# Layer 1 of a group's first two batches, spread over the last four attention slots through a spare PSUM bank

## The chip, the cores and the metric

The kernel runs on one core of a Trainium2 chip. Its engines are TensorE (PE in the profile, its weight loads PEld), VectorE (DVE), ScalarE (ACT), GpSimd (POOL) and SyncE (SP), which issues the DMAs. Each works off its own instructions in order and waits on semaphores. The metric is the device time of one execution in microseconds (us), lower is better.

## The reference, cut to what matters

There are 64 batches of 256 tokens with 256 features, and for each batch 120 context vectors. Attention has 16 heads of 16 features.

```python
x = x + attention(layernorm(x), ctx, mask) @ W_out.T    # softmax(10 * tanh(q k / 4)) v, masked keys out
f = layernorm(x)
gf = global_net(mean of f over the tokens)              # 3 small layers, one value per batch
out = f
for _ in range(3):
    h = gelu(out @ w1 + b1); h = gelu(h @ w2 + b2); h = gelu(h @ w3 + b3)
    tf = sigmoid(h @ w4 + b4)                           # one value per token
    coupling = 0.1 + adaptive_range * (0.7 * gf + 0.3 * tf - 0.5) * 2
    out = out + coupling * twist(out)                   # twist permutes and negates quarters of the features
x = x + out
```

## The kernel before

The batches are worked through in 8 groups of 8. For each batch there is an attention slot; after the eight slots that finish a group's features comes that group's feed-forward stage ("ffn", all three cycles for its 2048 tokens in 4 chunks of 2 batches), and then the next slots. The functions of every engine are called in a fixed order by a loop over `slots()`. In slot `i` the scores are made for batch `i`, the weighted values for `i-1`, the projection for `i-2`, and the second norm and the feature transpose for `i-3` (`LAG = 3`). The place of a slot in its group is `(i - LAG) % GROUP`, 0 to 7. The ffn stage of a group stands behind its place 7.

**Attention slot.** ScalarE: tanh of half of batch `i` (L880), exp of the second half of `i-1` (L886), tanh of the other half, exp, and `features` (L896), which writes `f_t` and the sum over tokens; in place 7 one more exp. TensorE: scores half 0 (L1116), weighted values half 0 (L1132), query transposes (L1091), scores half 1, projection half 0 (L1147), key transposes (L1100), weighted values half 1, projection half 1, feature transposes (L1160). A half of the scores takes all of the banks 0 to 3 and so waits for the tanh before it. VectorE: `attn_out` of half 0 (L678), `queries_out` (L664), stats, the combination of an output of the group before, `high_half` in places 2 and 4, `keys_out` (L669), `attn_out` of half 1, the division, a transpose, the residual and stats of `i-2`. GpSimd: the norms, two products per output of the group before (L511, L520), `query_hat` (L435), and last `low_half` (L529).

**Layer 1.** The first layer's product is taken once for each chunk and updated by linearity in the cycles: `u = w1' f` and `v = w1' twist(f)`. To be precise enough, `f` and the weights are split into two float16 parts each (`high_half` on VectorE, `low_half` on GpSimd, buffer `f_hl` with two slots) and three partial products are added in PSUM. `layer1_twisted` (L1179) makes `v` in banks 2 and 3, `layer1_straight` (L1192) makes `u` in banks 0 and 1, each 12 matmuls of 512 columns. `twisted_out` (L924) and `straight_out` (L934) on ScalarE scale them into `v_t` and, in place of the features, into `f_t`. `gelu1` (L912) of the first cycle reads PSUM, later ones read `f_t`.

**The head of an ffn stage.** TensorE: both products of chunk 0, the global net's first layer (L1254), the twisted product of chunk 1, the global net's second layer (L1258), layer 2 (L1205) of chunk 0, and so on. ScalarE: two evictions, two gelus (with a table load, as exp and gelu have different tables), two evictions, the global net's gelu (L999), the evictions of chunk 1. GpSimd: norms for queries of later batches, `low_half` of chunk 2, one more query, `low_half` of chunk 3.

Weighted values use banks 4 and 5, one for each half; layer 2 uses the same two in turn.

Of the kernel before, what the change touches and what calls it, by code (L numbers as in the profile page):

```python
# [35 lines left out]
P = 128  # L36
# [8 lines left out]
def xattn_ffn_kernel(nc, x, ctx, mask, W_out, scale, log_C,  # L45
# [30 lines left out]
    with ExitStack() as stack:  # L76
# [108 lines left out]
        PV_BANKS = (4, 5)  # L185
# [46 lines left out]
        s_uv = sem("s_uv")  # L232
        s_h1 = sem("s_h1")
# [17 lines left out]
        LOW_AT = (3, 4, 5, 6)  # L251
# [67 lines left out]
        def groups_before(i):  # L319

            return (i - LAG) // GROUP

# [261 lines left out]
        def _(eng):  # L584
# [88 lines left out]
            def attn_out(b, n):  # L673

                eng.wait_ge(s_pv, 2 * b + n + 1)
                if b >= 2:
                    eng.wait_ge(s_on, b - 1)
                eng.transpose(o_t[:, b % 2, 2 * n:2 * n + 2].rearrange("p c q r -> p (c q r)"),  # L678
                              banks(PV_BANKS[n])).then_inc(s_ot, 1)

# [45 lines left out]

            def couple(g, p):

                turn, chunk = UPDATES * g + p, slot_of(p)[1]
                eng.wait_ge(s_th, turn + 1)  # L730
                eng.wait_ge(s_gcs, g + 1)
                for b in range(CB):
                    c = coup[:, turn % 2, b * S:(b + 1) * S]
                    eng.tensor_scalar(c, c, c_tok[:, 0:1], c_batch[:, chunk * CB + b:chunk * CB + b + 1],  # L734
                                      ALU.mult, ALU.add).then_inc(s_coup, 1)

            def update_both(g, p):
# [5 lines left out]
                eng.wait_ge(s_uv, 2 * EK * (number + 1))  # L743
# [57 lines left out]
            for kind, i in slots():  # L801
                if i == 2 and kind == "attention":
                    split_weights()
                if kind == "attention":
# [16 lines left out]
                    if 0 <= nxt < NB:  # L821
                        keys_out(nxt)
                    if 0 <= here < NB:
                        attn_out(here, 1)
                        divide(here)
                        attn_features(here)
# [45 lines left out]
        def _(eng):  # L872
# [26 lines left out]
            def gelu1(g, p):  # L899
# [3 lines left out]
                for m in range(EK):  # L903
                    if cyc == 0:
                        eng.wait_ge(s_w, n_weights)
                        eng.wait_ge(s_vec0, N_SPLIT)
# [69 lines left out]
            for kind, i in slots():  # L976
# [15 lines left out]
                else:  # L992
                    early = i * GROUP + GROUP + LAG
                    glob = banks(TR_BANK)[:, SMALL_AT:SMALL_AT + 3 * GROUP]
                    twisted_out(i, 0)
                    gelu1(i, 0)
                    straight_out(i, 0)
# [53 lines left out]
        def _(eng):  # L1051
# [52 lines left out]
            def scores(b, n):  # L1104
# [3 lines left out]
                if n == 0 and after_ffn(b):  # L1108
                    eng.wait_ge(s_th, UPDATES * groups_before(b))
                    eng.wait_ge(s_uv, 2 * EK * CHUNKS * groups_before(b))  # L1110
                elif 2 * b + n:
                    eng.wait_ge(s_tanh, 2 * b + n)
# [8 lines left out]
            def weighted_values(b, n):  # L1121
# [3 lines left out]
                if after_ffn(b + 1):  # L1125
                    eng.wait_ge(s_h2, PASSES * groups_before(b + 1) - 1 + n)
                elif b:
                    eng.wait_ge(s_ot, 2 * (b - 1) + n + 1)
                for c in (2 * n, 2 * n + 1):
                    for j in range(HG):  # L1130
                        h = n * HALF + 2 * j + c % 2
                        last = eng.matmul(banks(PV_BANKS[n])[j * SLOT:(j + 1) * SLOT, (c % 2) * S:(c % 2 + 1) * S],  # L1132
# [33 lines left out]

            def layer1_twisted(g, chunk):
# [3 lines left out]
                eng.wait_ge(s_vec0, N_SPLIT)  # L1171
                eng.wait_ge(s_flo, EK * (number + 1))
                for m in range(EK):
                    if chunk == 0:
                        eng.wait_ge(s_tanh, 2 * min(GROUP * g + GROUP + LAG, NB))
                    else:
                        eng.wait_ge(s_uv, 2 * EK * (number - 1) + m + 1)
# [5 lines left out]
            def layer1_straight(g, chunk):  # L1183
# [3 lines left out]
                for m in range(EK):  # L1187
                    if chunk:
                        eng.wait_ge(s_h1, EK * (PASSES * g + chunk - 1) + m + 1)
                        eng.wait_ge(s_uv, 2 * EK * (number - 1) + EK + m + 1)  # L1190
# [5 lines left out]
            def layer2(g, p):  # L1196
# [4 lines left out]
                else:  # L1201
                    eng.wait_ge(s_ot, 2 * min(GROUP * g + GROUP + LAG - 1, NB))
                for k in range(EK):
# [15 lines left out]
            def layer4(g, p):  # L1219
# [7 lines left out]
                if paired(p):  # L1227
                    eng.wait_ge(s_uv, 2 * EK * CHUNKS * (g + 1))
# [36 lines left out]
            for kind, i in slots():  # L1265
                if kind == "attention":
# [3 lines left out]
                    if i != early:  # L1270
# [94 lines left out]
```

## Time and profile before

| | |
|---|---|
| median of 3 runs | 1096.31 us (1096.15 to 1098.32) |
| the profiled execution | 1098.4 us, its span 1096.6 us |
| TensorE busy | 979.9 us (89%), weight loads 530.3 us (48%) |
| ScalarE busy | 920.6 us (84%) |
| VectorE busy | 808.9 us (74%) |
| GpSimd busy | 554.1 us (51%) |
| chain that ended last | ScalarE 41%, TensorE 30%, issue 13%, VectorE 10% |
| mean granted clock of TensorE | 0.979 of full speed |

The shares are means over two alternating kinds of stage, attention and ffn, of some 67 and 63 us for a middle group, with different limits. The chain is followed back from the last instruction; "issue" is time for which the profile shows no wait.

### The profile page before, as it was taken

Reading aid. Unit: us, or ns where it says so; the run is one execution under the profiler, and the core shown is the slowest. Engines: PE = TensorE matmul, PEld = TensorE weight load, DVE = VectorE, ACT = ScalarE, POOL = GpSimd, SP = SyncE. Lnnn points to the kernel's source line nnn. Section 1 sums busy time; section 2 is a strip of 40 time slices with the busy share of each in tenths; the row PEclk is TensorE's granted clock in tenths of the full one; section 3 lists DMA queues with packets and bytes.
Section 4 is the critical chain, followed back from the end, with each engine's and each line's share of the span. In section 5 each row is a group of like instructions: output and inputs, shape, how many; then the busy total and the mean of one; then the engine's idle time right before and its main releaser. Section 6 shows DMA issues by size and latency. Waiting matters only on the chain.

```text
span 1096.6 us, 21849 instructions
## 1 busy us (share of the span) xinstructions
PE 979.9 (89%) x7260; PEld 530.3 (48%) x7260; DVE 808.9 (74%) x1738; ACT 920.6 (84%) x1153; POOL 554.1 (51%) x1053
## 2 busy tenths in 40 slices
PE   6899989899998999999999998989999899896993
PEld 4455435554355544554345543555435554453431
DVE  3888596985868666885869849698487867687285
ACT  3899778997799977998789977899779997795675
POOL 3367504884068810897028950488406881078104
PEclk7899999999999999999999999999999999998997
DMA  5433001430034200441005310143003420021002
GB/s 119 82 58 61 1 2 39 105 86 0 2 72 100 58 1 2 96 92 41 2 1 121 90 19 2 40 104 86 0 2 73 99 58 1 1 53 40 0 1 78
DMA packets 191119, 51.71 MB, mean 47 GB/s; under 512 B 165920, under 2 KB 174624, under 8 KB 191008
## 3 DMA queue, kind: packets, MB, share of 16 engines
q1 hardware_dynamic: 191008, 50.31, 21.6%
q8 instruction: 60, 0.98, 0.4%
q14 instruction: 51, 0.42, 0.1%
HBM read 33.37 MB, written 16.78 MB: 46 GB/s over the span
## 4 chain that ended last, share of the span: by engine, by line
ACT 41%; PE 30%; issue 13%; DVE 10%; SPq 2%; POOL 2%; DMA 1%; DVEq 0%; ACTq 0%; POOLq 0%
ACT probs L880 18%; ACT probs L886 14%; PE ps L1205 7%; PE ps L1192 6%; PE ps L1179 5%; ACT f_t L896 4%; PE ps L1116 3%; PE ps L1235 2%; DVE move_u L747 2%; DVE move_v L749 2%; PE ps L1214 2%; ACT h L912 2%; DVE f_t L753 2%; DVE coup L734 2%; PE ps L1147 1%
## 5 line engine op out<-in xcount | busy, mean ns | idle before, releaser
L880 ACT ACTIVATE probs<-ps,u_scale 120x2048 f32<-120x2048 f32 x128 | 257.6, 2012 | 21.4 <-PE ps L1116 21.4
L886 ACT ACTIVATE probs<-probs,exp_bias,clip 120x2048 f32<-120x2048 f32 x128 | 275.0, 2149 | 0.1
L1205 PE MATMUL ps<-h,w 128*128 128x512 f32 x384 | 184.4, 606 | 12.9 <-ACT h L912 12.1
L1116 PE MATMUL ps<-q_t,k_t 32*120 32x256 f32 x2048 | 150.0, 407 | 34.6 <-ACT probs L880 33.1
L475 POOL TENSOR_TENSOR c<-tok_c 128x16 f32<-128x16 f32 x8 | 1.8, 224 | 329.3 <-issue 329.3
L1147 PE MATMUL ps<-wo_t,of_t 128*128 128x256 f32 x512 | 144.5, 405 | 1.8 <-DVE xy L703 1.8
L678 DVE STREAM_TRANSPOSE o_t<-ps 128x512 f32<-128x512 f32 x128 | 90.8, 709 | 74.5 <-PE ps L1132 74.2
L1132 PE MATMUL ps<-probs,va 120*32 120x256 f32 x2048 | 138.4, 388 | 2.0 <-ACT probs L886 2.0
L1116 PEld LDWEIGHTS ps<-q_t,k_t 32*120 32x120 f32 x2048 | 95.1, 181 | 65.0 <-issue 60.5
L1147 PEld LDWEIGHTS ps<-wo_t,of_t 128*128 128x128 f32 x512 | 87.3, 190 | 51.0 <-issue 42.1
L1205 PEld LDWEIGHTS ps<-h,w 128*128 128x128 f32 x384 | 66.8, 188 | 87.7 <-issue 64.4
L942 ACT ACTIVATE h<-ps,b 128x512 f32<-128x512 f32 x96 | 65.6, 684 | 39.1 <-PE ps L1205 39.1
L912 ACT ACTIVATE h<-f_t,b 128x512 f32<-128x512 f32 x128 | 85.1, 715 | 11.6 <-DVE f_t L772 8.2
L1179 PE MATMUL ps<-f_hl,w1t_hl 128*128 128x512 f16 x384 | 90.1, 385 | 0.0
L734 DVE TENSOR_SCALAR coup<-coup,c_tok,c_batch 128x256 f32<-128x256 f32 x128 | 49.3, 427 | 54.7 <-ACT coup L966 53.6
L1192 PE MATMUL ps<-f_hl,w_hl 128*128 128x512 f16 x384 | 88.2, 379 | 0.0
L529 POOL TENSOR_TENSOR f_hl<-f_t,f_hl 128x512 f16<-128x512 f32 x64 | 75.2, 1186 | 19.9 <-DVE f_hl L725 19.9
L1132 PEld LDWEIGHTS ps<-probs,va 120*32 120x32 f32 x2048 | 53.8, 110 | 57.5 <-issue 19.5
L435 POOL TENSOR_SCALAR q_hat<-xy,neg,rstd 128x256 f32<-128x256 f32 x128 | 77.4, 613 | 4.2 <-POOL rstd L425 3.8
L456 POOL TENSOR_SCALAR f_hat<-xy,neg,rstd 128x256 f32<-128x256 f32 x128 | 74.4, 587 | 5.4 <-POOL rstd L446 5.4
L725 DVE CAST f_hl<-f_t 128x1024 f16<-128x1024 f32 x32 | 23.6, 738 | 70.0 <-PE ps L1192 70.0
L912 ACT ACTIVATE h<-ps,b,uv_scale 128x512 f32<-128x512 f32 x64 | 48.9, 776 | 31.2 <-PE ps L1192 31.1
(128 smaller groups left out, 1826.5 us busy)
## 6 DMA issues: line engine op xcount, KB each, us to landing
xy<-in_x_dram SPq DMA_DIRECT2D x64, 256.0 KB, 3.3
out_dram<-xy SPq DMA_DIRECT2D x64, 256.0 KB, 2.0
cbuf<-in_ctx_dram SPq DMA_DIRECT2D x64, 120.0 KB, 2.8
va<-in_ctx_dram SPq DMA_DIRECT2D x64, 120.0 KB, 3.6
tok_c<-coup SPq DMA_DIRECT2D x256, 0.5 KB, 2.0
move_v<-in_L_xattn_W_out_dram SPq DMA_DIRECT2D x1, 256.0 KB, 5.6
move_u<-in_L_ffn_cn_w_dram SPq DMA_DIRECT2D x1, 256.0 KB, 3.4
w<-in_L_ffn_cn_w_dram SPq DMA_DIRECT2D x1, 128.0 KB, 3.1
```

Source lines behind the costliest of these rows:

```text
L435: eng.tensor_scalar(q_hat[:, at, t, :], xy[:, b % XR, t * E:(t + 1) * E], neg1[:, at, t:t + 1], rstd1[:, at, t:t + 1], ALU.add, ALU.mult). ...
L529: eng.tensor_tensor(f_hl[:, slot, 1, k], f_t[:, k, tok], f_hl[:, slot, 0, k], ALU.subtract) \
L678: eng.transpose(o_t[:, b % 2, 2 * n:2 * n + 2].rearrange("p c q r -> p (c q r)"), banks(PV_BANKS[n])).then_inc(s_ot, 1)
L880: eng.activation(probs[:, b % 2, n * HALF:(n + 1) * HALF, :].rearrange("k h q -> k (h q)"), banks(SCORE_BANK, 4)[0:KEYS, :], ACT.Tanh, sca ...
L886: eng.activation(p, p, ACT.Exp, scale=clip[0:KEYS, 0:1], bias=exp_bias[:, b:b + 1]).then_inc(s_exp, 1)
L912: eng.activation(h1[:, p % 2, m, :], source, ACT.Gelu, bias=b1[:, m:m + 1], scale=by) \
L1116: last = eng.matmul(banks(SCORE_BANK + r)[0:KEYS, odd * S:(odd + 1) * S], k_t[rows, b % 2, odd, n, :], q_t[rows, b % 2, n, :], start=True, ...
L1132: last = eng.matmul(banks(PV_BANKS[n])[j * SLOT:(j + 1) * SLOT, (c % 2) * S:(c % 2 + 1) * S], va[:, b % VR, h, :], probs[:, b % 2, h, :], ...
L1147: last = eng.matmul(banks(X_BANK)[:, t * E:(t + 1) * E], of_t[:, k, t * P:(t + 1) * P], wo_t[:, k, :], start=(k == 0), stop=(k == EK - 1))
L1179: last = eng.matmul(banks(V_BANKS[m]), w1t_hl[:, w, k, m * P:(m + 1) * P], halves[:, f, k, :], start=(n == 0), stop=(n == len(PRODUCTS) - 1))
L1192: last = eng.matmul(banks(U_BANKS[m]), w1_hl[:, w, k, m * P:(m + 1) * P], halves[:, f, k, :], start=(n == 0), stop=(n == len(PRODUCTS) - 1))
L1205: last = eng.matmul(banks(bank), w2[:, k, :], h1[:, p % 2, k, :], start=(k == 0), stop=(k == EK - 1))
```

## The change

Chunk 0 of every group no longer gets its layer 1 in the ffn stage. Its four pieces (`v` and `u`, two halves of the features each: six matmuls and one eviction a piece) are made one by one in the attention slots of places 4 to 7, by `layer1_side` on TensorE between the queries and the second half of the scores, and by `side_out` on VectorE between `keys_out` and the second `attn_out`. They pass through bank 5. That bank is free because both halves of the weighted values now go through bank 4, each behind the transpose of the one before. `gelu1` of chunk 0 reads `f_t`; `twisted_out` and `straight_out` of chunk 0 (ScalarE) and both products of chunk 0 (TensorE) leave the head. The low halves of chunk 0 are made in places 2 and 3 instead of 3 and 4.

```diff
-        PV_BANKS = (4, 5)
+        PV_BANK = 4
+        SIDE_BANK = 5
...
         HIGH_AT = (2, 4)
-        LOW_AT = (3, 4, 5, 6)
+        LOW_AT = (2, 3, 5, 6)
+
+        SIDE_AT = (4, 5, 6, 7)
+        SIDES = 2 * EK
...
+        def uv_done(g, chunk):
+            return 2 * EK * ((CHUNKS - 1) * g + chunk)
...
+        def side_of(i):
+            at = (i - LAG) % GROUP
+            return SIDE_AT.index(at) if i >= LAG and at in SIDE_AT else None
...
+            def side_out(g, part):
+                kind, m = part // EK, part % EK
+                eng.wait_ge(s_vec0, N_SPLIT)
+                eng.wait_ge(s_l1, 2 * EK * CHUNKS * g + part + 1)
+                if g and kind == 0:
+                    eng.wait_ge(s_vupd, EK * (CHUNKS * (g - 1) + 1))
+                    eng.wait_ge(s_mvu, EK * (UPDATES * (g - 1) + CHUNKS + 1))
+                dst = (v_t, f_t)[kind]
+                eng.tensor_scalar(dst[:, m, 0:CT], banks(SIDE_BANK), uv_scale[:, 0:1], None, ALU.mult).then_inc(s_side, 1)
...
                     if 0 <= nxt < NB:
                         keys_out(nxt)
+                    if side_of(i) is not None:
+                        side_out((i - LAG) // GROUP, side_of(i))
                     if 0 <= here < NB:
                         attn_out(here, 1)
...
                 for m in range(EK):
-                    if cyc == 0:
+                    if cyc == 0 and chunk == 0:
                         eng.wait_ge(s_w, n_weights)
-                        eng.wait_ge(s_vec0, N_SPLIT)
+                        eng.wait_ge(s_side, SIDES * (g + 1))
+                        source, by = f_t[:, m, 0:CT], 1.0
+                    elif cyc == 0:
                         eng.wait_ge(s_l1, 2 * EK * (CHUNKS * g + chunk) + EK + m + 1)
                         source, by = banks(U_BANKS[m]), uv_scale[:, 0:1]
...
                     glob = banks(TR_BANK)[:, SMALL_AT:SMALL_AT + 3 * GROUP]
-                    twisted_out(i, 0)
                     gelu1(i, 0)
-                    straight_out(i, 0)
...
                 eng.wait_ge(s_va[b % VR], 16 * (b // VR + 1))
-                if after_ffn(b + 1):
-                    eng.wait_ge(s_h2, PASSES * groups_before(b + 1) - 1 + n)
-                elif b:
-                    eng.wait_ge(s_ot, 2 * (b - 1) + n + 1)
+                if after_ffn(b + 1) and n == 0:
+                    eng.wait_ge(s_h2, PASSES * groups_before(b + 1) - 1)
+                if 2 * b + n:
+                    eng.wait_ge(s_ot, 2 * b + n)
...
+            def layer1_side(g, part):
+                kind, m = part // EK, part % EK
+                halves = f_hl[:, CHUNKS * g % 2]
+                weights = (w1t_hl, w1_hl)[kind]
+                if part == 0:
+                    eng.wait_ge(s_vec0, N_SPLIT)
+                    eng.wait_ge(s_flo, EK * (CHUNKS * g + 1))
+                if part == 0 and g:
+                    eng.wait_ge(s_h2, PASSES * g)
+                elif part:
+                    eng.wait_ge(s_side, SIDES * g + part)
+                for n, (w, f, k) in enumerate(PRODUCTS):
+                    last = eng.matmul(banks(SIDE_BANK), weights[:, w, k, m * P:(m + 1) * P], halves[:, f, k, :],
+                                      start=(n == 0), stop=(n == len(PRODUCTS) - 1))
+                last.then_inc(s_l1, 1)
...
                         if 0 <= nxt < NB:
                             queries(nxt)
+                        if side_of(i) is not None:
+                            layer1_side((i - LAG) // GROUP, side_of(i))
                         if 0 <= i < NB:
                             scores(i, 1)
...
                     early = i * GROUP + GROUP + LAG
-                    layer1_twisted(i, 0)
-                    layer1_straight(i, 0)
                     global_net(i, 0)
```

The other lines of the diff fit the counts of `s_uv`, which chunk 0 no longer raises, let chunk 1's products wait for the last tanh alone, and let layer 2's first two products and the first update wait for `s_side`.

## Rows read from the trace of the kernel before

**Rows 1.** Windows: a stretch's us, then busy us (instructions) of each engine

```profile
core 0: us, PE busy (x) PEld busy (x) DVE busy (x) ACT busy (x) POOL busy (x), PEclk, DMA share, GB/s
338.20:346.59 8.39, 7.55 (x90) 4.83 (x86) 7.31 (x17) 8.39 (x10) 8.01 (x14) 1.00 0.52 126
381.50:388.66 7.16, 7.16 (x35) 3.72 (x36) 0.83 (x2) 5.19 (x9) 5.81 (x11) 1.00 0.01 3
...
1016.00:1018.00 2.00, 2.00 (x6) 0.76 (x5) 0.00 (x0) 0.27 (x2) 0.00 (x0) 0.50 0.00 0
```

**Rows 2.** Timeline of TensorE, places 4 to 7 of group 2: start, us, engine, line

```profile
338.88 0.66 PE L1091 MATMUL ps<-ident,q_hat 128*128 128x128 f32 x4
340.37 1.14 PE L1116 MATMUL ps<-q_t,k_t 32*120 32x256 f32 x16 [0.84 <-ACT probs L880]
...
348.78 1.14 PE L1116 MATMUL ps<-q_t,k_t 32*120 32x256 f32 x16 [0.85 <-ACT probs L880]
...
356.42 0.66 PE L1091 MATMUL ps<-ident,q_hat 128*128 128x128 f32 x4 [0.66 <-POOL q_hat L435]
...
364.94 0.66 PE L1091 MATMUL ps<-ident,q_hat 128*128 128x128 f32 x4 [0.77 <-POOL q_hat L435]
```

**Rows 3.** Timeline of ScalarE: place 7 and head of group 2, last features

```profile
367.20 2.10 ACT L880 ACTIVATE probs<-ps,u_scale 120x2048 f32<-120x2048 f32 x1
...
373.74 1.41 ACT L924 ACTIVATE v_t<-ps,uv_scale 128x512 f32<-128x512 f32 x2
375.17 1.28 ACT L912 ACT_TABLE_LOAD   x1
376.46 1.45 ACT L912 ACTIVATE h<-ps,b,uv_scale 128x512 f32<-128x512 f32 x2
377.80 1.26 ACT L934 ACTIVATE f_t<-ps,uv_scale 128x512 f32<-128x512 f32 x2
378.94 0.28 ACT L999 ACTIVATE gh<-ps,gb 128x8 f32<-128x8 f32 x1
...
1015.80 0.38 ACT L896 ACTIVATE f_t<-ps 128x256 f32<-128x256 f32 x1
```

**Rows 4.** Timeline of TensorE, the head of group 2

```profile
370.34 2.75 PE L1179 MATMUL ps<-f_hl,w1t_hl 128*128 128x512 f16 x12
372.93 2.75 PE L1192 MATMUL ps<-f_hl,w_hl 128*128 128x512 f16 x12
...
379.49 1.98 PE L1205 MATMUL ps<-h,w 128*128 128x512 f32 x4
...
385.00 2.76 PE L1179 MATMUL ps<-f_hl,w1t_hl 128*128 128x512 f16 x12
```

**Rows 5.** Groups of instructions by line: busy us and mean ns behind the bar

```profile
L912 ACT ACTIVATE h<-f_t,b 128x512 f32<-128x512 f32 x128 | 85.1, 715 | 11.6 <-DVE f_t L772 8.2 <-PE ps L1205 3.4
...
L912 ACT ACTIVATE h<-ps,b,uv_scale 128x512 f32<-128x512 f32 x64 | 48.9, 776 | 31.2 <-PE ps L1192 31.1
```

**Rows 6.** Timeline of VectorE, place 7 of group 2

```profile
365.69 0.65 DVE L664 COPY q_t<-ps 128x512 f32<-128x512 f32 x1
...
369.08 0.72 DVE L678 STREAM_TRANSPOSE o_t<-ps 128x512 f32<-128x512 f32 x1 [0.37 <-PE ps L1132]
```

**Rows 7.** Timeline of GpSimd, place 3 of group 2 to its head

```profile
333.50 0.32 POOL L422 TENSOR_SCALAR var<-mv 128x2 f32<-128x2 f32 x1 [0.59 <-DVE mv L658]
...
339.55 1.15 POOL L529 TENSOR_TENSOR f_hl<-f_t,f_hl 128x512 f16<-128x512 f32 x1
...
379.69 2.27 POOL L529 TENSOR_TENSOR f_hl<-f_t,f_hl 128x512 f16<-128x512 f32 x2
```

**Rows 8.** Timeline of TensorE, place 7 of group 0 and head of group 7

```profile
105.29 1.14 PE L1116 MATMUL ps<-q_t,k_t 32*120 32x256 f32 x16 [0.85 <-ACT probs L880]
...
1015.18 4.62 PE L1179 MATMUL ps<-f_hl,w1t_hl 128*128 128x512 f16 x12
...
1025.53 1.98 PE L1205 MATMUL ps<-h,w 128*128 128x512 f32 x4
```

More of the change, by code:

```diff
@@ L232, in xattn_ffn_kernel @@
         s_uv = sem("s_uv")
+        s_side = sem("s_side")
         s_h1 = sem("s_h1")
@@ L678, in attn_out @@
                 eng.transpose(o_t[:, b % 2, 2 * n:2 * n + 2].rearrange("p c q r -> p (c q r)"),
-                              banks(PV_BANKS[n])).then_inc(s_ot, 1)
+                              banks(PV_BANK)).then_inc(s_ot, 1)
             def divide(b):
@@ L742, in update_both @@
                 eng.wait_ge(s_coup, CB * (turn + 1))
-                eng.wait_ge(s_uv, 2 * EK * (number + 1))
+                if chunk == 0:
+                    eng.wait_ge(s_side, SIDES * (g + 1))
+                else:
+                    eng.wait_ge(s_uv, uv_done(g, chunk))
                 eng.wait_ge(s_upd, EK * turn)
@@ L903, in gelu1 @@
                 for m in range(EK):
-                    if cyc == 0:
+                    if cyc == 0 and chunk == 0:
                         eng.wait_ge(s_w, n_weights)
-                        eng.wait_ge(s_vec0, N_SPLIT)
+                        eng.wait_ge(s_side, SIDES * (g + 1))
+                        source, by = f_t[:, m, 0:CT], 1.0
+                    elif cyc == 0:
                         eng.wait_ge(s_l1, 2 * EK * (CHUNKS * g + chunk) + EK + m + 1)
@@ L1109, in scores @@
                     eng.wait_ge(s_th, UPDATES * groups_before(b))
-                    eng.wait_ge(s_uv, 2 * EK * CHUNKS * groups_before(b))
+                    eng.wait_ge(s_uv, uv_done(groups_before(b), 0))
                 elif 2 * b + n:
@@ L1131, in weighted_values @@
                         h = n * HALF + 2 * j + c % 2
-                        last = eng.matmul(banks(PV_BANKS[n])[j * SLOT:(j + 1) * SLOT, (c % 2) * S:(c % 2 + 1) * S],
+                        last = eng.matmul(banks(PV_BANK)[j * SLOT:(j + 1) * SLOT, (c % 2) * S:(c % 2 + 1) * S],
                                           va[:, b % VR, h, :], probs[:, b % 2, h, :], start=True, stop=True,
@@ L1170, in layer1_twisted @@
                 halves = f_hl[:, number % 2]
-                eng.wait_ge(s_vec0, N_SPLIT)
                 eng.wait_ge(s_flo, EK * (number + 1))
                 for m in range(EK):
-                    if chunk == 0:
+                    if chunk == 1:
                         eng.wait_ge(s_tanh, 2 * min(GROUP * g + GROUP + LAG, NB))
                     else:
-                        eng.wait_ge(s_uv, 2 * EK * (number - 1) + m + 1)
+                        eng.wait_ge(s_uv, uv_done(g, chunk - 2) + m + 1)
                     for n, (w, f, k) in enumerate(PRODUCTS):
@@ L1187, in layer1_straight @@
                 for m in range(EK):
-                    if chunk:
+                    if chunk > 1:
                         eng.wait_ge(s_h1, EK * (PASSES * g + chunk - 1) + m + 1)
-                        eng.wait_ge(s_uv, 2 * EK * (number - 1) + EK + m + 1)
+                        eng.wait_ge(s_uv, uv_done(g, chunk - 2) + EK + m + 1)
                     for n, (w, f, k) in enumerate(PRODUCTS):
@@ L1202, in layer2 @@
                     eng.wait_ge(s_ot, 2 * min(GROUP * g + GROUP + LAG - 1, NB))
+                    eng.wait_ge(s_side, SIDES * (g + 1))
                 for k in range(EK):
@@ L1227, in layer4 @@
                 if paired(p):
-                    eng.wait_ge(s_uv, 2 * EK * CHUNKS * (g + 1))
+                    eng.wait_ge(s_uv, uv_done(g, CHUNKS - 1))
                 for b in range(CB):
```

## The prediction

> **What bounds the kernel now.** I read the windows of a stretch of one middle group first, then the timelines of TensorE, ScalarE, GpSimd and VectorE over it. I call an attention slot by its place, 0 to 7, in its group; in the group of the rows, places 4 to 7 begin at 338.20, 346.59, 354.98 and 363.37 us and the last ends at 371.75. In place 4 ScalarE is busy for all of 8.39 us [rows 1]: attention is bound by it, and what delays it there is never made up. TensorE is next. Its steps follow each other without a gap, but for one wait a slot: 0.84 and 0.85 us for a tanh in places 4 and 5, 0.66 and 0.77 us for q_hat in places 6 and 7 [rows 2]. VectorE too is nearly full. In the feed-forward stage TensorE is busy for the whole of 381.50 to 388.66 [rows 1]. Between the two lies a head of ScalarE work: two evictions, a table load, two gelus, two evictions, then the global net's first gelu, for which TensorE waits before layer 2 at 379.49 [rows 3, 4].
>
> **What the change takes out.** Of ScalarE's head it takes the two evictions at 373.74 (to 375.17: 1.43 us) and the two at 377.80 (to 378.94: 1.14 us) [rows 3]. The gelus read f_t instead of PSUM: 715 ns against 776 ns in the line groups [rows 5], so 0.12 us for two. Together 2.69 us. On TensorE 24 matmuls leave the head, but that time was not limiting there: TensorE began them at 370.34, before ScalarE was through with exp at 373.74, and still waited for ScalarE later. So a middle group's head saves 2.69 us, not the 5.2 us of matmuls. After layer 2 the order is the old one and bound by TensorE, so what the head gives lasts.
>
> **What it adds to the slots.** (a) TensorE: six matmuls of 512 columns in each of places 4 to 7. From the start of twelve at 370.34 to that of the next twelve at 372.93 pass 2.59 us [rows 4] (the 2.75 us of the row hold a modelled tail), so six cost 1.30 us. They stand between the queries and the second half of the scores, just where TensorE waits today. (b) VectorE: one 128x512 scaling out of PSUM, 0.65 us by the q_t copy of that shape [rows 6]; it stands after keys_out and ahead of attn_out, where VectorE waits 0.37 us for TensorE [rows 6]. Alone it would just fit. (c) The weighted values in one bank wait for the transpose of the other half, but that is no new wait: VectorE makes it before the queries_out for which the key transposes wait, and the second half of the weighted values stands behind these. In the first slot after a feed-forward stage VectorE has nothing else to do. So nothing. Had it no such cover, each wait would be one 0.72 us transpose. (d) The low halves of chunk 0 move on GpSimd: they are made in places 2 and 3 instead of 3 and 4, at 1.15 us each [rows 7]; chunk 1's stay.
>
> **The low half that comes late.** layer1_side's part 0, in place 4, waits for both low halves of chunk 0. GpSimd works them off at the end of its queue for a slot, behind the two norms, the previous group's outputs and q_hat. In a middle group the one of place 3 starts at 339.55 and ends at 340.70 [rows 7], long into place 4, and the one now in place 2 stands ahead of it: 1.24 us with the gap behind it, of which the 0.59 us that GpSimd waits for VectorE at 333.50 [rows 7] cover a part. So it ends at about 341.35. TensorE is done with its queries at 339.54 and today goes on at 340.37 [rows 2]. It now holds, with everything queued behind it, until 341.4, runs the side part until 342.7 and only then gives the scores: 2.33 us late. Before this change nothing in the slot hung on that low half. No DMA is added, and SyncE's queue is untouched; its loads only follow the later slots.
>
> **The sum for a middle group.** After place 4 TensorE is 2.33 us late and has no idle left but its one wait a slot. Place 5: +1.30 - 0.85, 2.78 late. Place 6: q_hat comes later as well, since GpSimd waits in place 5 for VectorE, which is some 2.5 us behind by then. It is due at 356.4 + 2.5 = 358.9, and TensorE asks for it at 356.42 - 0.66 + 2.78 = 358.5, so of the 0.66 us some 0.36 remain as a wait: +1.30 - 0.30, 3.78 late. Place 7: +1.30 - 0.77, 4.3 late. The last scores of place 7 are today ready 0.4 us before their tanh at 367.20 (364.94 + 0.66 + 1.14 = 366.74) [rows 2, 3], so ScalarE ends its attention 3.9 us late. Less 2.69 us that is +1.2 us. One thing more: low_half of chunk 2 follows stats on VectorE, which follow TensorE's last slot; with VectorE 4.5 us late, the pair that ends at 381.96 [rows 7] ends at 386.45, while the twisted product of chunk 2 (385.00 today [rows 4]) would be due at 386.2. That makes it +1.5 us. There are six such groups: +9.0 us.
>
> **The first and the last group.** In group 0 GpSimd has no outputs of an earlier group to make and the low halves are in time; TensorE waits 0.85 us for tanh in each of the four slots (one of them in [rows 8]). It falls behind by 4 x 0.45 = 1.8 us, ScalarE by 1.4, the head gives back 2.69, but chunk 2's low half, 2.0 us later than today, leaves some 0.7 us: -0.7. In the last group three of the four slots have no scores; the chain there runs over VectorE and GpSimd, and the side parts fall into TensorE's idle time. Today the head after it is bound by TensorE: 24 matmuls from 1015.18 on, the first ones at half clock (the granted clock there is 0.50, the 1.2 GHz level [rows 1]), until layer 2 at 1025.53 [rows 8]. Afterwards the features end at 1016.3 [rows 3], then come the global product (0.6) and twelve matmuls of the twisted product of chunk 1, which would take between 12 x 0.22 = 2.6 us and twice that, cold. I take a mix, 4.3: layer 2 at 1021.5, -4.0 us.
>
> **Total.** +9.0 - 0.7 - 4.0 = +4.3 us on the profiled span of 1096.6 us, 1100.9 us. The profiled execution took 1098.4 us, the median of the runs is 1096.31 us, so nearer the span: 1096.31 + 4.3, I say 1100.5 us.
>
> **A rule against my sum.** TensorE is busy for 7.55 of 8.39 us with matmuls, but only 4.83 us (58%) with weight loads [rows 1]. The Trainium skill, in Perfetto Trace Analysis, section Identifying the Most-Contended Engine, says that busy matmuls are no good measure for TensorE and that the busy share of its weight loads is a better one. By it over a third of the slot would be open, and the side parts would cost nothing but the wait for the low half.
>
> **Rivals.** (1) TensorE has room. The side parts hide, place 4 costs only the hold to 341.4, 1.0 us on TensorE and 0.6 on ScalarE; a middle group gains 2.1, group 0 2.7, the last 4: 1096.3 - 19 = 1077 us. For it stands only the low share of the weight loads; against it that each step takes the same time, 1.14 us for a half of the scores, whether TensorE waited before it or not [rows 2]. This is the case of the rule. Chance 0.03. (2) The low half is in time or nearly. Then TensorE is late by 0.46, 0.92, 1.8 and 2.35 us, ScalarE by 2.0, and a middle group gains 0.5 to 0.7: 6 x -0.5 - 4.7 = -7.7, 1088.6 us. It decides for faster as soon as the low half ends before 339.9; the row says 340.7 even without the new backlog. Chance 0.08. (3) The terms are right in kind, but smaller in the middle groups (+0.8 for one, if waits overlap more than I add up): 4.8 - 4.7, no change. This needs half of my 1.5 us to be wrong. Chance 0.17. (4) More is lost: VectorE's extra op and the waits for q_hat add up over the slots, another 0.6 us in each of two slots, 2.7 us a middle group: 16.2 - 4.7 = +11.5, 1107.8 us. For it speaks that VectorE is busy for 7.31 of 8.39 us [rows 1] and gets 0.65 us more. Chance 0.10. My forecast: 0.62.
>
> **Bounds and chances.** Unknown are the side part's cost between other kinds of matmul (1.2 to 1.5 us), the low half's end (340.9, were the 0.59 us to cover more, to 341.7), and the last group (-3.1 at 1.2 GHz throughout, -5.7 at 2.4). Low ends: 6 x 0.5 - 0.9 - 5.7 = -3.6; high ends: 6 x 2.2 - 0.5 - 3.1 = +9.6. With a part of rivals 2 and 4 the range is 1093.5 to 1107. A difference under 0.2% (2.2 us) can't be told from none here. Faster by more: rivals 1 and 2 and a little of 3, 0.13. The same: most of 3 and the low edge of the forecast, 0.17. Slower: 0.70.
>
> **What would show it.** In the middle groups TensorE should wait some 1.8 us for GpSimd ahead of the first side part, not for ScalarE; ScalarE should show idle time before tanh, about 3.9 us over places 4 to 7, growing from slot to slot; groups 1 to 6 should each be 1 to 2 us longer and the last head 4 us shorter. In the head ScalarE should go from exp to the table load at once. I am wrong if the first side part starts at once behind the queries, or if TensorE is found idle in places 5 to 7 while ScalarE is still full.

## The result, and the profile after

The changed kernel takes 1101.32 us (median of 5 runs, 1100.77 to 1101.92), the kernel before 1096.96 us beside it (5 runs, 1096.15 to 1098.32): ratio 1.0039, 95% interval 1.0024 to 1.0053. That is 4.4 us slower, little but clear of the noise; the forecast was 4.3 us more, 1100.5 us. The profiled execution took 1100.87 us, its span 1099.0 us; the profiled spans differ by only 2.4 us, since the start-up up to group 0's place 1 happened to take 1.3 us longer in the trace of before (that tanh starts at 52.72 us there and at 51.40 after).

To see where it went I cut both traces at two instructions of ScalarE, which occur once a group: the token-wise tanh that ends a feed-forward stage (L1004 after) and the global net's first gelu in the head (L1029 after; L999 before). All times are differences of start times.

| stretch, us | before | after | difference | forecast |
|---|---|---|---|---|
| start to group 0's gelu | 118.63 | 115.99 | -2.64, of it -1.3 start-up | -1.3 |
| rest of the stage, group 0 | 59.09 | 58.77 | -0.3 | +0.6 |
| attention and head, a middle group | 71.24 (six, within 0.01) | 72.84 to 72.89 (five), 72.47 | +1.6 | +1.2 |
| rest of the stage, a middle group | 58.74, in three 58.86 to 59.35 | 58.77 (six, within 0.01) | 0 but for the three | +0.3 |
| six middle groups, both stretches | 781.06 | 789.35 | +8.3 | +9.0 |
| last group, both stretches | 123.04 | 120.25 | -2.8 | -4.0 |

The low half of chunk 2, which the forecast charged with 0.3 us in a middle group and 0.6 in group 0, stands behind the global gelu and so in the second stretch. The stages that are longer in the trace of before (group 0 and three middle ones) wait there for the transfer of the token coefficients (tok_c) ahead of a tanh; the three make up 1.2 us of that sum. In the trace of after such a wait of 0.59 us stands in group 6 alone and lengthens nothing. Now the rows, of group 2 again. Everything up to TensorE's wait for f_hat in place 3 (the first row below) is 1.33 us earlier than in [rows 1 to 7], so a time of after is compared with one of before by adding 1.33. First TensorE in places 3 to 7 and the head (start, us, engine, line; in brackets the idle time ahead of it and who ended it):

```profile
335.40 0.66 PE L1190 MATMUL ps<-ident,f_hat 128*128 128x128 f32 x4 [0.29 <-POOL f_hat L470]
...
338.05 0.66 PE L1121 MATMUL ps<-ident,q_hat 128*128 128x128 f32 x4
340.32 1.46 PE L1210 MATMUL ps<-f_hl,w1t_hl 128*128 128x512 f16 x6 [1.61 <-issue]
341.70 1.14 PE L1146 MATMUL ps<-q_t,k_t 32*120 32x256 f32 x16
...
350.49 1.14 PE L1146 MATMUL ps<-q_t,k_t 32*120 32x256 f32 x16
...
357.91 0.66 PE L1121 MATMUL ps<-ident,q_hat 128*128 128x128 f32 x4 [0.44 <-POOL q_hat L449]
...
359.79 1.14 PE L1146 MATMUL ps<-q_t,k_t 32*120 32x256 f32 x16
...
366.95 0.66 PE L1121 MATMUL ps<-ident,q_hat 128*128 128x128 f32 x4 [0.19 <-POOL q_hat L449]
...
368.83 1.14 PE L1146 MATMUL ps<-q_t,k_t 32*120 32x256 f32 x16
...
379.56 0.28 PE L1305 MATMUL ps<-gh,g 128*64 128x8 f32 x2 [1.56 <-ACT gh L1029]
379.77 1.98 PE L1252 MATMUL ps<-h,w 128*128 128x512 f32 x4
```

In place 4 TensorE stands still for 1.61 us ahead of the first side part. The profile calls it "issue", it has no releaser for it; what ended it is on GpSimd:

```profile
330.23 1.16 POOL L543 TENSOR_TENSOR f_hl<-f_t,f_hl 128x512 f16<-128x512 f32 x1
...
339.05 1.17 POOL L543 TENSOR_TENSOR f_hl<-f_t,f_hl 128x512 f16<-128x512 f32 x1
```

The second low half ends at 340.22 and the side part starts at 340.32. In the frame of before that end is at 341.55; forecast 341.35. From there on the waits for tanh of [rows 2] are gone. ScalarE, whose tanhs waited nowhere in these four places of group 2 before, does so now:

```profile
337.19 1.97 ACT L910 ACTIVATE probs<-ps,u_scale 120x2048 f32<-120x2048 f32 x1 [0.15 <-PE ps L1146]
...
342.91 1.97 ACT L910 ACTIVATE probs<-ps,u_scale 120x2048 f32<-120x2048 f32 x1 [1.77 <-PE ps L1146]
...
361.00 1.97 ACT L910 ACTIVATE probs<-ps,u_scale 120x2048 f32<-120x2048 f32 x1 [0.51 <-PE ps L1146]
...
374.61 2.09 ACT L916 ACTIVATE probs<-probs,exp_bias,clip 120x2048 f32<-120x2048 f32 x1
376.72 1.28 ACT L944 ACT_TABLE_LOAD   x1
378.02 1.33 ACT L944 ACTIVATE h<-f_t,b 128x512 f32<-128x512 f32 x2
379.26 0.25 ACT L1029 ACTIVATE gh<-ps,gb 128x8 f32<-128x8 f32 x1
```

The last exp starts 4.2 us late (374.61 + 1.33 against 371.75), but from the table load to the global gelu only two gelus are left; the evictions of [rows 3] between them are gone, and the first two now come behind it, at 379.41. A window of 8.79 us (so long is a slot of TensorE that waits for nothing, experiment 6) over its work for place 5 shows it without a gap:

```profile
core 0: us, PE busy (x) PEld busy (x) DVE busy (x) ACT busy (x) POOL busy (x), PEclk, DMA share, GB/s
...
346.84:355.63 8.79, 8.79 (x92) 5.34 (x88) 7.97 (x20) 8.63 (x10) 4.94 (x11) 1.00 0.22 44
```

The page's line of groups and its chain say the same for the whole kernel: the tanhs stand idle for 38.7 us, 38.0 of it for the scores, where the page of before has 21.4 us, and TensorE has taken first place in the chain from ScalarE (42% against 30% before).

```profile
PE 42%; DVE 19%; POOL 14%; issue 12%; ACT 10%; SPq 2%; DVEq 0%; DMA 0%; POOLq 0%; ACTq 0%
...
L910 ACT ACTIVATE probs<-ps,u_scale 120x2048 f32<-120x2048 f32 x128 | 252.9, 1976 | 38.7 <-PE ps L1146 38.0
```

### The profile page after: what moved, and what is told of

It is laid out like the page before. It is cut to its first block, busy times and chain, and to the rows that moved or that the text cites. A ratio compares the mean times of both kernels' runs of the same rounds, so it can differ in the third digit from the quotient of the medians.

```text
span 1099.0 us, 21815 instructions
## 1 busy us (share of the span) xinstructions
PE 979.5 (89%) x7260; PEld 525.0 (48%) x7260; DVE 827.3 (75%) x1770; ACT 907.4 (83%) x1121; POOL 576.7 (52%) x1053
## 4 chain that ended last, share of the span: by engine, by line
PE 42%; DVE 19%; POOL 14%; issue 12%; ACT 10%; SPq 2%; DVEq 0%; DMA 0%; POOLq 0%; ACTq 0%
PE ps L1146 7%; PE ps L1252 6%; PE ps L1177 5%; PE ps L1225 4%; PE ps L1162 4%; PE ps L1238 4%; ACT probs L910 4%; PE ps L1210 3%; ACT probs L916 2%; POOL q_hat L449 2%; POOL rstd L439 2%; DVE move_u L796 2%; PE ps L1282 2%; POOL f_hl L543 2%; DVE move_u L775 2%
## 5 line engine op out<-in xcount | busy, mean ns | idle before, releaser
L910 ACT ACTIVATE probs<-ps,u_scale 120x2048 f32<-120x2048 f32 x128 | 252.9, 1976 | 38.7 <-PE ps L1146 38.0
L916 ACT ACTIVATE probs<-probs,exp_bias,clip 120x2048 f32<-120x2048 f32 x128 | 268.6, 2099 | 0.1
L1146 PEld LDWEIGHTS ps<-q_t,k_t 32*120 32x120 f32 x2048 | 91.5, 178 | 56.8 <-issue 50.9
L944 ACT ACTIVATE h<-f_t,b 128x512 f32<-128x512 f32 x144 | 95.7, 715 | 13.5 <-DVE f_t L800 9.4
L470 POOL TENSOR_SCALAR f_hat<-xy,neg,rstd 128x256 f32<-128x256 f32 x128 | 95.1, 750 | 5.4 <-POOL rstd L460 5.4
L683 DVE TENSOR_TENSOR k_t<-ps,parity 128x480 f32<-128x480 f32 x64 | 41.9, 655 | 48.0 <-PE ps L1130 48.0
L449 POOL TENSOR_SCALAR q_hat<-xy,neg,rstd 128x256 f32<-128x256 f32 x128 | 72.1, 573 | 4.2 <-POOL rstd L439 3.8
L525 POOL TENSOR_SCALAR twisted<-xy,neg,b_r 128x256 f32<-128x256 f32 x112 | 70.7, 642 | 1.2 <-POOL x_add L489 1.1
L534 POOL TENSOR_SCALAR xy<-xy,x_fac,x_add 128x256 f32<-128x256 f32 x112 | 70.8, 644 | 0.0
L1225 PE MATMUL ps<-f_hl,w1t_hl 128*128 128x512 f16 x288 | 68.4, 389 | 0.5
```

What stands on the lines that cost most here:

```text
L449: eng.tensor_scalar(q_hat[:, at, t, :], xy[:, b % XR, t * E:(t + 1) * E], neg1[:, at, t:t + 1], rstd1[:, at, t:t + 1], ALU.add, ALU.mult). ...
L470: eng.tensor_scalar(f_hat[:, t, :], xy[:, at, t * E:(t + 1) * E], neg2[:, at, t:t + 1], rstd2[:, at, t:t + 1], ALU.add, ALU.mult).then_inc ...
L910: eng.activation(probs[:, b % 2, n * HALF:(n + 1) * HALF, :].rearrange("k h q -> k (h q)"), banks(SCORE_BANK, 4)[0:KEYS, :], ACT.Tanh, sca ...
L916: eng.activation(p, p, ACT.Exp, scale=clip[0:KEYS, 0:1], bias=exp_bias[:, b:b + 1]).then_inc(s_exp, 1)
L944: eng.activation(h1[:, p % 2, m, :], source, ACT.Gelu, bias=b1[:, m:m + 1], scale=by) \
L1146: last = eng.matmul(banks(SCORE_BANK + r)[0:KEYS, odd * S:(odd + 1) * S], k_t[rows, b % 2, odd, n, :], q_t[rows, b % 2, n, :], start=True, ...
```

## The experiments

I write "middle group" for the time from token tanh to global gelu in groups 1 to 6: 71.24 us before, 72.85 after. Each ratio is to the kernel before, with its 95% interval.

**1. The low half of place 3 first in GpSimd's queue.** The theory says that its place in the queue, not its cost, makes the loss.

```diff
                     norm_2(i - LAG)
+                if i >= LAG and (i - LAG) % GROUP == 3:
+                    low_half((i - LAG) // GROUP, 0, 1)
                 if after_ffn(i):
...
-                if i >= LAG and (i - LAG) % GROUP in LOW_AT:
+                if i >= LAG and (i - LAG) % GROUP in LOW_AT and (i - LAG) % GROUP != 3:
```

> The changed kernel, but in place 3 GpSimd makes the low half right behind the second norm, ahead of the products and q_hat. Theory (the first side part waits for that low half, and from there on TensorE has no slack to win the time back): the hold of 1.6 us ahead of the first side part goes, TensorE ends place 7 of a middle group some 2.4 us late instead of 4.6, so each middle group is 2.0 us shorter than in the changed kernel; 6 x 2.0 = 12, about 1089 us where before stands at 1097. Rival (the side matmuls themselves fill TensorE, the hold is only where the time shows): the wait moves to later slots, and the time stays within 2 us of 1101.

Measured 1090.14 us (5 runs), ratio 0.9937 (0.9923 to 0.9950). The middle group takes 71.15 us, 1.70 less than in the changed kernel; six times that is 10.2 of the 11.2 us won. I had expected 2.0 us a group. It is also less than rival 2 of the prediction, the low half in time, which promised a group 0.5 to 0.7 us shorter than before: it is 0.1 us shorter, and TensorE still waits 0.30 us for f_hat in place 3 and 0.73 us for q_hat in place 6. TensorE and GpSimd in place 4:

```profile
337.39 0.65 PE L1123 MATMUL ps<-ident,q_hat 128*128 128x128 f32 x4
337.88 1.46 PE L1212 MATMUL ps<-f_hl,w1t_hl 128*128 128x512 f16 x6
```

```profile
334.64 1.17 POOL L543 TENSOR_TENSOR f_hl<-f_t,f_hl 128x512 f16<-128x512 f32 x1
```

The half is ready at 335.81, two us before it is wanted, and the hold is gone. One instruction's order decides the sign of the whole change.

**2. The same low half later instead of earlier.** If the hold is this wait, moving its producer one place further back must make it far worse.

```diff
-        LOW_AT = (2, 3, 5, 6)
+        LOW_AT = (3, 4, 5, 6)
```

> The changed kernel with the low halves in places 3, 4, 5, 6 as they were before, so that the second low half of chunk 0 ends behind the outputs of place 4. Theory: it ends 6.4 us later in a middle group, and TensorE holds for that much more; 6 x 6 = 36, with some 7 more in group 0 and some 6 in the last group about 1150 us. Rival (TensorE's load decides and not the hold): the later slots absorb most of it, below 1115 us.

Measured 1168.01 us (one run), a middle group 79.4 to 81.3 us. The hold is 7.44 us, 5.8 more than in the changed kernel, and a group is 6.5 to 8.8 us longer; I had expected 6. At least a part of the rest is the clock: behind the hold TensorE runs at half of it.

```profile
364.51 2.72 PE L1210 MATMUL ps<-f_hl,w1t_hl 128*128 128x512 f16 x6 [7.44 <-issue]
```

```profile
360.00:364.00 4.00, 0.00 (x0) 0.00 (x0) 0.00 (x0) 0.00 (x0) 3.95 (x7) 0.55 0.76 162
364.00:367.00 3.00, 2.49 (x6) 0.74 (x6) 0.00 (x0) 0.00 (x0) 0.40 (x1) 0.50 0.00 0
```

TensorE, VectorE and ScalarE all stand still from 360 to 364; the granted clock is 0.50 (the 1.2 GHz level) behind that, and the side part takes 2.72 us instead of 1.46.

**3. The kernel before with one bank for the weighted values.** This part alone, without the layer 1.

```diff
-        PV_BANKS = (4, 5)
+        PV_BANK = 4
...
-                elif b:
-                    eng.wait_ge(s_ot, 2 * (b - 1) + n + 1)
+                if 2 * b + n:
+                    eng.wait_ge(s_ot, 2 * b + n)
```

> The kernel before with one change, both halves of the weighted values in bank 4. Theory: no new wait ends last, as VectorE frees the bank before TensorE asks for it; within 1 us of before, 1097. Rival (the shared bank ties TensorE to VectorE's transposes and is a part of the loss): 0.1 to 0.3 us in each of 64 slots, 1103 to 1115 us.

Measured 1097.39 us (11 runs), ratio 1.0004 (0.9995 to 1.0013); a middle group 71.20 us against 71.24. The bank costs nothing there, and the page of the changed kernel puts none of the idle time ahead of its weighted values to VectorE.

**4. One product of six in the side parts.** It tells whether TensorE was full in the slots, or had room and merely seemed busy.

```diff
-                for n, (w, f, k) in enumerate(PRODUCTS):
+                for w, f, k in PRODUCTS[:1]:
```

> The changed kernel with one matmul of six in each side part; the other five products of chunk 0's first layer are left out. All waits stay. Theory: the hold in place 4 stays (TensorE 1.6 us idle ahead of the part, ScalarE about 1.6 us late), but places 5 to 7 add nothing, as 0.22 us fit into TensorE's wait of 0.66 to 0.85; ScalarE ends attention some 1.7 us late instead of 4.2, a middle group is 2.5 us shorter; 1101 - 15 - 1 = 1085 us. Rival (TensorE has room for all six, by its share of weight loads, and only the hold costs): no difference but the hold's end, 1098 to 1101 us.

Measured 1086.44 us (4 runs), ratio 0.9901 (0.9887 to 0.9914); a middle group 70.37 us, 2.5 less than with all six. Had TensorE had room, the products would have cost nothing and their absence gained nothing. The rest of the 4.3 us of matmul time that is gone (20 at 0.216) turns into other waits: the hold in place 4 is as in the changed kernel, in place 6 TensorE waits for q_hat, and in place 5 it waits for tanh again:

```profile
337.09 0.38 PE L1210 MATMUL ps<-f_hl,w1t_hl 128*128 128x512 f16 x1 [1.59 <-issue]
...
345.55 1.14 PE L1146 MATMUL ps<-q_t,k_t 32*120 32x256 f32 x16 [0.38 <-ACT probs L910]
...
353.66 0.66 PE L1121 MATMUL ps<-ident,q_hat 128*128 128x128 f32 x4 [1.03 <-POOL q_hat L449]
```

So either cost stands without the other: the hold stays without the products, and the products cost without the hold (experiment 6).

**5. VectorE's new operation cut to one column** (in groups 1 to 7).

```diff
-                eng.tensor_scalar(dst[:, m, 0:CT], banks(SIDE_BANK), uv_scale[:, 0:1], None, ALU.mult).then_inc(s_side, 1)
+                wide = 1 if g else CT
+                eng.tensor_scalar(dst[:, m, 0:wide], banks(SIDE_BANK)[:, 0:wide], uv_scale[:, 0:1], None, ALU.mult).then_inc(s_side, 1)
```

> The changed kernel with side_out on one column instead of 512 in groups 1 to 7; the rest of chunk 0's v_t and f_t keeps old values there. VectorE gets back 0.5 us in each of the four slots, nothing else changes. Theory (TensorE and the hold set the time, VectorE only follows): what can be won is the q_hat wait left in places 6 and 7, which hangs on VectorE, at most 0.5 us a group: 1098 to 1100 us. Rival (VectorE is the second bound of the slots and its extra op a main part of the loss): 4 x 0.5 = 2 us a group, 1089 us.

Measured 1099.66 us (8 runs), ratio 1.0024 (1.0014 to 1.0034); a middle group 72.6 us. Cut to one column an operation takes 208 instead of 742 ns, so VectorE is spared 2.1 us a group, and the group is 0.25 us shorter: VectorE follows TensorE. Its row in the changed kernel shows why. It waits 2.71 us for the keys ahead of this operation, for TensorE has just been held:

```profile
344.15 0.66 DVE L683 TENSOR_TENSOR k_t<-ps,parity 128x480 f32<-128x480 f32 x1 [2.71 <-PE ps L1130]
```

**6. q_hat too goes ahead of the outputs of the previous group**, on top of experiment 1.

```diff
                     coefficients(groups_before(i) - 1)
+                if new is not None and 2 <= new < NB:
+                    query_hat(new)
                 for b in late[:2] if after_ffn(i) else late[:1]:
...
-                if new is not None and 2 <= new < NB:
-                    query_hat(new)
```

> e1 with one more step on GpSimd: query_hat stands ahead of the products for the previous group's outputs in every slot. Theory: the wait of 0.73 us for q_hat that TensorE still has in place 6 goes, and TensorE's slots of places 4 to 7 are all 8.79 us; 0.7 us a middle group, 1086 us. Rival (it moves to f_hat, the outputs or the stores): no better than e1, 1090 us.

Measured 1087.37 us (5 runs), ratio 0.9916 (0.9902 to 0.9929); a middle group 70.33 us, 0.82 less than in experiment 1, where q_hat still held TensorE for 0.73 us in place 6. Expected were 0.7 us. Now TensorE has no wait left in places 4 to 7, and the side parts show its own rhythm:

```profile
335.83 1.46 PE L1212 MATMUL ps<-f_hl,w1t_hl 128*128 128x512 f16 x6
...
344.61 1.46 PE L1212 MATMUL ps<-f_hl,w1t_hl 128*128 128x512 f16 x6
```

These two are 8.78 us apart, the next two 8.79 each, against ScalarE's 8.39 [rows 1]. Even without a single late input each of the four slots loses 0.40 us to TensorE.

**7. Half the work in the slots**, on top of experiment 6: only the twisted pieces, three matmuls in each place; the straight ones stay in the head.

```diff
-                for n, (w, f, k) in enumerate(PRODUCTS):
+                for n, (w, f, k) in list(enumerate(PRODUCTS))[3 * second:3 * second + 3]:
```

> e6, but only the two twisted pieces of chunk 0 go through the side bank, three matmuls in each of places 4 to 7, and are scaled out in places 5 and 7; the straight product, its two evictions and a gelu from PSUM stay in the head. Theory: three matmuls (0.65 us) fit into TensorE's wait of a slot, so ScalarE has no idle in attention at all, and the head is shorter by the two evictions, 1.43 us: a middle group 128.6 us against 130.1 before, the last one some 3 us shorter; 1084 us. Rival (any side work ahead of the scores costs its full time): a middle group at 130.5 or more, 1095 us or more.

A miss: 1090.41 us (5 runs), ratio 0.9942 (0.9930 to 0.9955). The slots did what the theory says; with three matmuls ScalarE's tanhs are 8.38 us apart again. But a middle group takes 70.31 us (one 70.94), a gain of 0.93 over before instead of the 1.43 of the two evictions. Some 0.3 of that is lost in place 3, where TensorE waits for f_hat, which GpSimd makes late because of the low half in place 2 (without that half, in experiment 9, this wait is gone). The other 0.2 us stand ahead of the table load:

```profile
368.62 2.17 ACT L919 ACTIVATE probs<-probs,exp_bias,clip 120x2048 f32<-120x2048 f32 x1
370.81 1.28 ACT L945 ACT_TABLE_LOAD   x1
```

From the last exp to the table load pass 2.19 us; before, from that exp (371.75) to the first eviction (373.74, [rows 3]) only 1.99. The table load starts when the instruction ahead of it has ended, an eviction starts a little earlier, and the 1.43 us of the two evictions held that difference. The rest of the stage is longer in three of the middle groups. Two of them, by 0.9 and 0.5 us, have a wait for tok_c. In the third it is the clock, with a granted 0.60 in 763 to 767 us: layer 2 takes 3.66 instead of 1.98 us, and that is as much as its whole excess of 1.7 us.

```profile
763.79 3.66 PE L1256 MATMUL ps<-h,w 128*128 128x512 f32 x4
```

**8. The head alone.** The kernel before, with chunk 0's layer 1 in the head cut to one of six products and evictions of one column from group 1 on. It shows what the head is worth when nothing is put into the slots.

```diff
-                    for n, (w, f, k) in enumerate(PRODUCTS):
+                    used = PRODUCTS if chunk or not g else PRODUCTS[:1]
+                    for n, (w, f, k) in enumerate(used):
```

> The kernel before with chunk 0's layer 1 shortened in the head for groups 1 to 7: one matmul of six in each of its four products, and its four evictions on one column; the rest of the work is left out, and nothing is added to the slots. Theory: the head's share of the change alone, on ScalarE 4 x 0.4 = 1.6 to 2.0 us a group (an eviction of one column still costs some 0.2 us), and some 4 us in the last group: 1097 - 6 x 1.8 - 4 = 1082 us. Rival (the head was bound by TensorE's 24 matmuls): 5.2 - 0.9 = 4.3 us a group, 1067 us.

Measured 1087.55 us (4 runs), ratio 0.9919 (0.9905 to 0.9932), against 1082 expected. Up to the global gelu a middle group gains 1.73 us (69.51), as expected: the head is worth ScalarE's time there and not TensorE's 5.2 us. But in five of six the rest of the stage then takes 59.51 to 60.07 us instead of 58.74. TensorE, with little left to do ahead of it, makes the next twisted product in 4.44 us instead of 2.75. The windows show the granted clock fall to 0.50. In group 5 the same product, behind the same wait of 1.61 us, kept its clock, and this is the one middle group whose rest of the stage takes 58.74 us:

```profile
370.95 0.61 PE L1258 MATMUL ps<-f_sum,g 128*128 128x8 f32 x4 [0.69 <-ACT f_t L896]
373.17 4.44 PE L1182 MATMUL ps<-f_hl,w1t_hl 128*128 128x512 f16 x12 [1.61 <-ACT v_t L925]
...
761.40 2.75 PE L1182 MATMUL ps<-f_hl,w1t_hl 128*128 128x512 f16 x12 [1.61 <-ACT v_t L925]
```

```profile
371.00:373.00 2.00, 0.56 (x4) 0.47 (x4) 1.97 (x9) 2.00 (x3) 0.00 (x0) 1.00 0.38 139
373.00:375.00 2.00, 1.83 (x6) 0.77 (x7) 1.90 (x8) 1.97 (x4) 1.60 (x4) 0.66 0.00 0
375.00:377.00 2.00, 2.00 (x7) 0.61 (x5) 0.60 (x4) 1.98 (x6) 1.83 (x5) 0.50 0.00 0
```

**9. Both low halves of chunk 0 in place 3, right behind norm_2**, on top of experiment 6.

```diff
                 if i >= LAG and (i - LAG) % GROUP == 3:
-                    low_half((i - LAG) // GROUP, 0, 1)
+                    for k in range(EK):
+                        low_half((i - LAG) // GROUP, 0, k)
...
-                if i >= LAG and (i - LAG) % GROUP in LOW_AT and (i - LAG) % GROUP != 3:
+                if i >= LAG and (i - LAG) % GROUP in LOW_AT[2:]:
```

> e6 with both low halves of chunk 0 in place 3, right behind the second norm, so that place 2 has none. Theory: in the changed kernel, e1, e6 and e7 GpSimd carries a backlog from place 2 to place 3, so TensorE waits 0.29 us for f_hat there and ScalarE's next tanh comes 0.3 us late; that goes in six groups, and the low halves still end a microsecond before TensorE asks for them: 0.3 to 0.4 us a middle group, 1085.5 us against 1087.4 for e6. Rival (the pair now comes late for place 4): the hold is back, 1088 us or more.

Measured 1086.79 us (4 runs), ratio 0.9908 (0.9894 to 0.9921); a middle group 69.94 us, 0.39 less than in experiment 6, as expected, and the wait for f_hat is gone. The whole times of the two can't be told apart, since the intervals overlap. Its median is the lowest here of a version that does all the work, 0.9% below the kernel before.

**10. Sixteen matmuls that nothing reads, behind the last side part**, in the changed kernel. It tests the last group alone: was it the clock that kept the gain of the last head below the forecast?

```diff
                             layer1_side((i - LAG) // GROUP, side_of(i))
+                        if i == NB + LAG - 1:
+                            for _ in range(16):
+                                eng.matmul(banks(0), w1_hl[:, 0, 0, 0:P], w1_hl[:, 0].rearrange("p k e -> p (k e)"),
+                                           start=True, stop=True)
```

> The changed kernel with 16 more matmuls, whose result nothing reads, behind the last side part of the last group, into bank 0. Theory (the last head saves less than forecast as TensorE's clock falls to 1.2 GHz in the 4.5 us of idle time ahead of it): the twisted product of chunk 1 takes 2.6 instead of 4.9 us and layer 2 of the last group comes 2 to 2.3 us earlier; 1099.0 us against 1101.3. Rival (the clock falls anyway, or ScalarE's table load and gelus bind there): no difference, 1101 us.

Measured 1098.37 us (11 runs), ratio 1.0015 (1.0006 to 1.0024), 2.9 us less than the changed kernel for more work; in the trace both stretches of the last group take 117.41 instead of 120.25 us. The last head in the changed kernel with its clock, then here:

```profile
1020.40 0.85 PE L1190 MATMUL ps<-ident,f_hat 128*128 128x128 f32 x4 [4.54 <-POOL f_hat L470]
1022.18 1.02 PE L1301 MATMUL ps<-f_sum,g 128*128 128x8 f32 x4 [0.93 <-ACT f_t L926]
1023.05 4.96 PE L1225 MATMUL ps<-f_hl,w1t_hl 128*128 128x512 f16 x12
...
1028.15 1.99 PE L1252 MATMUL ps<-h,w 128*128 128x512 f32 x4
```

```profile
1021.00:1027.00 6.00, 5.07 (x16) 2.34 (x15) 0.00 (x0) 4.30 (x9) 1.58 (x2) 0.50 0.00 0
```

```profile
1016.31 3.62 PE L1328 MATMUL ps<-w_hl 128*128 128x512 f16 x16
1021.00 0.66 PE L1190 MATMUL ps<-ident,f_hat 128*128 128x128 f32 x4 [1.07 <-POOL f_hat L470]
...
1023.06 2.75 PE L1225 MATMUL ps<-f_hl,w1t_hl 128*128 128x512 f16 x12
...
1025.95 1.98 PE L1252 MATMUL ps<-h,w 128*128 128x512 f32 x4
```

## Why the prediction was right, step by step

**The low half that comes late** was the step on which the sign hung, and it held: forecast end 341.35, measured 341.55 in the same frame; a hold of 1.8 us forecast, 1.61 measured. Experiments 1 and 2 move the producer both ways and the time follows it both ways, by -11 and +67 us.

**TensorE is full behind it.** The second half of the scores was forecast 2.33, 2.78, 3.78 and 4.3 us late in places 4 to 7. It is 2.66, 3.04, 3.93 and 4.56 late (341.70 + 1.33 - 340.37, and so on). The difference arises in place 4, mostly 0.2 us at the low half and 0.08 in the side part, and some 0.2 us of it is still there in place 7. Six matmuls cost 1.38 us up to the scores (340.32 to 341.70), forecast 1.30; from place 5 on 0.17 us of it is made up ahead of the side part, which starts 0.49 us behind the queries where the scores came 0.66 behind them. A wait that I had left out, 0.29 us for f_hat in place 3 (the low half in place 2 pushes GpSimd's whole queue back, f_hat too), makes ScalarE 0.3 us late in place 4 already, but the hold covers it. The wait for q_hat left in place 6 was forecast at 0.36 and is 0.44 us; in place 7, where none was forecast, 0.19 us are left.

**ScalarE** loses 4.2 us where 3.9 were forecast. The idle times ahead of its tanhs add up to only 3.2 us; the rest is overlap that an instruction that must wait no longer has (the tanh at 351.70 starts 2.09 us behind the exp ahead of it, the features at 355.55, which need not wait, 1.99 us behind theirs). The idle column understates such a loss; starting times don't. The prediction also had these idle times grow from slot to slot, and there it was wrong: they are 1.9 us in place 4, then 0.2, 0.7 and 0.4.

**The head** gives back what ScalarE was spared, 2.7 us: its first instruction is 4.3 us late (376.72 + 1.33 against 373.74 in [rows 3]), layer 2 is 1.6 us late (379.77 + 1.33 against 379.49 in [rows 4]). The last 0.3 us of the forecast, the low half of chunk 2 that holds its twisted product, was nearly empty:

```profile
383.09 2.27 POOL L543 TENSOR_TENSOR f_hl<-f_t,f_hl 128x512 f16<-128x512 f32 x2
```

```profile
385.42 2.76 PE L1225 MATMUL ps<-f_hl,w1t_hl 128*128 128x512 f16 x12
```

The pair ends at 385.36 and the product starts at 385.42, 1.75 us late, so it costs some 0.15 there, and by the end of the stage 0.03 are left of it (58.77 against 58.74). That a group comes out at 1.6 against 1.5 is therefore partly luck: 0.4 us more than forecast at layer 2, 0.3 less behind it.

**The bank** cost nothing (experiment 3), **VectorE** followed (experiment 5), at 742 ns an operation instead of my 650.

**The rule on weight loads.** In place 5 the weight loads of TensorE are busy for 5.34 of 8.79 us, 61%, while it has no gap at all, and experiment 4 gives 2.5 us a middle group for the five products left out. The Trainium skill (Perfetto Trace Analysis, section Identifying the Most-Contended Engine) has the headroom of TensorE judged by that share and by the FLOP utilisation, which was not worked out here; rival 1, read from the weight loads alone, stood at 1077 us. The trace does not agree for this mix of small matmuls, and the measurement decides. What the prediction set against the rule was right, but its [rows 2] did not show it, since both halves of the scores there had waited; the halves at 341.70 and 350.49 waited for nothing and take the same 1.14 us.

**Two terms were mis-sized, and luck brought the total close.** The last group gave 2.8 us and not 4.0, which is outside the bounds of the prediction (3.1 with TensorE at 1.2 GHz throughout, 5.7 at 2.4). I had put the twisted product at 4.3 us, between cold and warm; up to layer 2 it took 5.1, as the clock was at 0.50 from 1021 to 1027 us, behind 4.54 us without a matmul; the global product ahead of it was cold as well, 0.87 us to the next start; and the features came 0.5 us later. Experiment 10 gives the clock's part, 2.8 us of this group; with it the group is 5.6 us shorter than before, close to the bound for 2.4 GHz.

The other term is the low half of chunk 2: it was to cost 0.3 us in each middle group and 0.6 in group 0, and cost next to nothing. Up to its gelu group 0 gave 1.3 us net of the start-up, as forecast. The middle groups lost 8.3 us and not 9.0, only because three waits for tok_c lengthen the trace of before and none that of after; against six without them it would be 9.5. With all such waits and the start-up left out, the terms of the traces add up to 5.4 us; the medians differ by 4.4. The terms offset each other in part, so the total is closer to the forecast than its terms.

Open is why waits for tok_c lengthen some groups of some executions and not others, how much of the 1 us between 5.4 and 4.4 is theirs, and why the clock fell in five middle groups of experiment 8 and not in the sixth.

## What to carry to other kernels

When work moves into the gaps of a nearly full engine, first look up where in its producer's queue the new input is made: here one instruction's place on GpSimd decided between 0.4% slower and 0.6% faster. Then add the moved work to the receiving engine's slot time and compare it with the bound: 8.79 against 8.39 us means a loss of 0.4 us a slot, whatever the idle columns say, to be set against what the stage it leaves really waited for (ScalarE's 2.7 us here, not TensorE's 5.2). And work taken off TensorE ahead of a stage that it bounds may have to be paid back in clock, as in experiment 8 and in the last group.

## What the runs showed of the hardware

The clock was less forgiving than I had thought. It was granted at 0.50 behind 7.4 us without a matmul (experiment 2) and behind 4.5 us (the last head), but also in experiment 8, where TensorE was busy for 0.56 us of the 2 us before it began to fall; there the rest of the stage was 0.8 to 1.3 us longer in five groups, and in a sixth with the same wait ahead the clock stayed. Sixteen matmuls that nothing reads, 3.62 us in all, kept it at the 2.4 GHz level through 1.07 us of waiting and the head behind it, and won 2.9 us. The Trainium skill (TensorE: Matmul & The Clock Gate, section Why this matters for your kernels) says that the layout of the loops decides whether the matmuls stay at the high clock; the trace agrees in so far as the same twelve matmuls took 4.96 us behind a wait, and 2.75 us when sixteen others had been put into that wait.

The order of instructions on ScalarE has a price too: a table load started only at the end of the exp ahead of it (2.19 us after its start, experiment 7), an eviction 1.99 us after it.
